# Value side first: reordering the work between the layers of a four-layer cross-attention kernel

## The reference, cut to what matters

```python
x = x + L0_xattn(layernorm(x), ctx, ...); x = x + L0_moe(layernorm(x), ...)    # top 2 of 8 experts
x = x + L1_xattn(layernorm(x), ctx, ...); x = x + L1_moe(layernorm(x), ...)    # top 1
x = x + L2_xattn(layernorm(x), ctx, ...); x = x + L2_ffn(layernorm(x), ...)    # gated, ternary weights
x = x + L3_xattn(layernorm(x), ctx, ...); x = x + L3_moe(layernorm(x), ...)    # top 1
# an attention: q = x @ Wq; k, v = ctx @ Wkv; softmax(q k^T * scale) v @ Wo + bo
```

## Time and profile before

| | us |
|---|---|
| median of 3 runs | 1031.07 (1029.62 to 1031.18) |
| profiled execution, whole | 1035.98 |
| its span, first to last instruction | 1033.6 |
| TensorE busy | 810.7 (78%) |
| VectorE busy | 600.9 (58%) |
| ScalarE busy | 485.4 (47%) |
| mean granted TensorE clock | 0.876 |

### The profile page before, as it was taken

The page is one execution under the profiler, slowest core; times in us unless marked ns, Lnnn a source line. Parts: engine busy times, 40 slices in busy tenths (PEclk is TensorE's granted clock), DMA queues, the critical chain, the costliest instruction groups (busy, mean ns, idle before and its releaser), DMA issues.

```text
span 1033.6 us, 15493 instructions
## 1 busy us (share of the span) xinstructions
PE 810.7 (78%) x4449; PEld 623.9 (60%) x4449; DVE 600.9 (58%) x2077; ACT 485.4 (47%) x1575; POOL 304.1 (29%) x396
## 2 busy tenths in 40 slices
PE   3887885599477888679956799889999777774794
PEld 1665675488345667557744577738668645563573
DVE  4756665487385788335436787452231258887574
ACT  2977752354175677124514445354443254441252
POOL 3100305367032355213401345300010113563142
PEclk9999987799797899669968899989999887885797
DMA  5032002333320000021110000000000300001213
GB/s 191 1 128 84 22 3 74 101 99 88 134 88 21 1 11 12 11 71 55 40 59 8 24 1 1 1 0 1 1 1 1 146 17 1 12 11 36 55 56 99
DMA packets 38642, 45.69 MB, mean 44 GB/s; under 512 B 7248, under 2 KB 31056, under 8 KB 37792
## 3 DMA queue, kind: packets, MB, share of 16 engines
q1 hardware_dynamic: 31344, 33.32, 10.0%
q0 software_dynamic: 4768, 9.91, 2.9%
q10 hardware_dynamic: 2448, 1.49, 0.5%
HBM read 31.92 MB, written 12.77 MB: 43 GB/s over the span
## 4 chain that ended last, share of the span: by engine, by line
PE 56%; DVE 24%; ACT 8%; issue 5%; DMA 4%; POOL 1%; SPq 1%; ACTq 0%; DVEq 0%; POOLq 0%
PE bank L940 8%; PE bank L834 7%; PE bank L897 6%; PE bank L915 5%; PE bank L807 5%; PE bank L832 4%; PE bank L767 4%; DVE s_xn L1082 3%; PE bank L818 3%; PE bank L906 3%; DVE s_peak L1105 2%; PE bank L756 2%; DVE s_total L1116 2%; PE bank L789 2%; ACT s_S L1572 1%
## 5 line engine op out<-in xcount | busy, mean ns | idle before, releaser
L807 PE MATMUL bank<-s_A,s_xTq 128*128 128x462 f32 (+1 forms) x352 | 157.6, 540 | 25.4 <-DVE s_S L1102 13.4
L1724 POOL TENSOR_TENSOR s_S<-s_S,s_inv 128x462 f32<-128x462 f32 (+1 forms) x128 | 105.1, 837 | 186.7 <-DVE s_inv L1119 185.4
L818 PE MATMUL bank<-s_ident,s_S 128*128 128x128 f32 (+2 forms) x560 | 97.4, 297 | 30.9 <-POOL s_S L1724 10.8
L818 PEld LDWEIGHTS bank<-s_ident,s_S 128*128 128x128 f32 (+2 forms) x560 | 71.6, 150 | 78.2 <-issue 37.2
L834 PEld LDWEIGHTS bank<-s_VW,s_PT 128*128 128x128 f32 (+2 forms) x800 | 111.7, 222 | 8.9 <-issue 7.7
L1757 POOL DMA_INDIRECT ys_L<-s_yo,s_yi x85 | 81.4, 957 | 121.3 <-DVE s_yo L1357 51.3
L834 PE MATMUL bank<-s_VW,s_PT 128*128 128x128 f32 (+2 forms) x800 | 114.4, 305 | 1.9 <-DVE s_x L1136 1.9
L1592 ACT ACTIVATE s_PT<-bank 128x384 f32<-128x384 f32 (+1 forms) x176 | 81.6, 470 | 64.6 <-PE bank L818 64.4
L789 PE MATMUL bank<-s_ident,s_xn 128*128 128x128 f32 x128 | 27.1, 353 | 84.3 <-DVE s_xn L1082 71.8
L1630 ACT ACTIVATE s_hT<-bank,s_b1T 128x128 f32<-128x128 f32 x184 | 52.7, 368 | 77.0 <-PE bank L906 76.9
L1750 POOL DMA_INDIRECT xs_L<-s_xn,s_sli x64 | 62.6, 977 | 88.8 <-DVE s_sli L1221 72.1
(11 more groups left out here) (214 smaller groups left out, 1733.0 us busy)
## 6 DMA issues: line engine op xcount, KB each, us to landing
s_xe<-xs_L SPq DMA_DIRECT2D x85, 66.0 KB
s_moe<-in_L_w SPq DMA_DIRECT2D x2, 2048.0 KB, 11.4
s_yb<-ys_L SPq DMA_DIRECT2D x16, 256.0 KB, 3.0
s_moe<-in_L_w SPq DMA_DIRECT2D x8, 512.0 KB, 7.0
s_arena<-in_L_w SPq DMA_DIRECT2D x2, 1024.0 KB, 5.9
s_arena<-in_L_h SPq DMA_DIRECT2D x2, 1024.0 KB, 9.1
ys_L<-s_yo,s_yi POOLq DMA_INDIRECT x85, 2.3
s_b2bc<-in_L_b SPq DMA_DIRECT2D x2, 512.0 KB, 5.8
```

What stands on the lines that cost most here:

```text
L807: mm(bank[b][:, 0:(h1 - h0) * KEYS], xTq_of(L, n)[:, i % 4, :], A[:, n, h0 * KEYS:h1 * KEYS], start=True, stop=True).then_inc(scores.up(L, ...
L818: w = turn(bank[b][0:m, P * (t - t0):P * (t - t0) + P], S[s][:, P * t:P * t + m], ident)
L1724: p.tensor_tensor(val, val, rep(inv[s][:, h0:h1], KEYS, 2), ALU.mult).then_inc(normed.up(L, i, k), 1)
```

## The change

For layers 2 and 3 (L = 1, 2) a new function `values_and_rows` writes the pieces in this order: the backs; products and folds of the value side; the combs; norm steps 0 and 1; three `vwt` pieces; norm steps 2 to 7; three `vwt` pieces; `xt`; the last six `vwt` pieces. The `vwt` pieces of these two layers are moved out by ScalarE for the first three batches and by VectorE for the last one; before, the two engines took them alternately. In the last layer this stays as it was. The attention's value matmuls wait for all pieces of their batch by name, where they waited for the last two.

For the last layer the key side is put alternately with norm and xt: product, norm step 0, fold 0, norm step 1, fold 1, norm step 2, and so on to fold 7, xt. The value side follows.

```diff
+    def values_and_rows(L):
+
+        side_work = keyside(L, 0)
+        vwt = [p for p in side_work if p[0] == "vwt"]
+        norm = [p for p in norm_rows("q", L, 0) if not isinstance(p, int)]
+        for piece in [*backs(L - 1, 0), *(p for p in side_work if p[0] != "vwt"), *combs(L - 1, 0), *norm[:2],
+                      *vwt[:3], *norm[2:], *vwt[3:6], ("xt", "q", L, 0), *vwt[6:]]:
+            put(*piece)
...
     experts(0)
-    woven(before(1, 0), [])
-    for piece in keyside(1, 0):
-        put(*piece)
+    values_and_rows(1)
     put("load", "L2v")
     put("load", "L2w")
...
     experts(1)
-    woven(before(2, 0), [])
-    for piece in keyside(2, 0):
-        put(*piece)
+    values_and_rows(2)
     put("load", "L3v")
...
     put("load", "L3w")
-    woven(before(3, 0), [])
-    for v in (1, 0):
-        for piece in keyside(3, v):
-            put(*piece)
+    woven(keyside(3, 1), before(3, 0))
+    for piece in keyside(3, 0):
+        put(*piece)
...
+    def on_dve_vwt(L, n, q):
+        return (n * len(spans(L)) + q) % 2 == 1 if L == 3 else n == NB - 1
...
-        mine = [(n, nq - 1), (n, nq - 2) if nq > 1 else (n - 1, 0)]
-        return [vwt_left(L, a, b) for a, b in mine if a >= 0]
+        return [vwt_left(L, n, q) for q in range(nq)]
```

More of the change, by code:

```diff
@@ L590, in body @@
     fold_dve = signal("fold_dve", (a for a in events("fold") if a[1] == 0 and a[2] % 2 == 0))
-    vwt_dve = signal("vwt_dve", (a for a in events("vwt") if (a[1] * len(spans(a[0])) + a[2]) % 2))
+    vwt_dve = signal("vwt_dve", (a for a in events("vwt") if on_dve_vwt(*a)))
     variance, scale_made, rows = signal("variance", "ln", 1), signal("ln_scale", "ln", 5), None
@@ L618, in body @@
     fold_act = signal("fold_act", (a for a in events("fold") if a[1] == 1 or a[2] % 2))
-    vwt_act = signal("vwt_act", (a for a in events("vwt") if not (a[1] * len(spans(a[0])) + a[2]) % 2))
+    vwt_act = signal("vwt_act", (a for a in events("vwt") if not on_dve_vwt(*a)))
     deviation = signal("deviation", "ln", 2)
@@ L688, in s_left @@
         return probs.at(L, i, k)
-    def on_dve_vwt(L, n, q):
-        return (n * len(spans(L)) + q) % 2 == 1
     def vwt_left(L, n, q):
```

## The result

The changed kernel took 998.42 us in the median (992.19 to 1000.27, 4 runs) against 1031.12 of the kernel before in the same comparison: a ratio of 0.9674, interval 0.9629 to 0.9719. The forecast was 1004.5: a gain of 26.6 us where 32.7 and then, by the second ratio, some 39 were measured. The time lies at the fast end of the range, that of the second ratio (0.9624 x 1031.12 = 992.4) beyond it.

A forecast was written before the change was run, and what follows sets the result against it. The prediction took TensorE's idle stretches in front of layers 2, 3 and 4 as the bound. Savings of 12.7 + 11.8 + 6.4, less 4.3 for the clock, gave 26.6 us: 1031.07 - 26.6 = 1004.5, range 998 to 1013.

The forecast's parts named there:

- What bounds the kernel: In front of layers 2, 3 and 4, TensorE stands idle (13.7 us at layer 2) before work that needs nothing of x.
- Products and folds straight behind the experts, at full clock: Layers 2 and 3: products follow the last expert matmul at once; first fold 3.11 us behind it.
- The transfer is hidden: Layers 2 and 3: fetched results land 2.7 and 5.4 us before VectorE asks for them, covered by the folds.
- Rows' transpose: Starts at 274.23 in layer 2; at 534.95 in layer 3, with 0.65 us lost to ScalarE's evictions.
- Scores in layers 2 and 3: First scores at 277.8 instead of 290.50 and 538.5 instead of 550.31, saving 12.7 and 11.8 us.
- the clock term: At the three starts, a lower granted clock costs between nothing and 12.8 us in all; a third, 4.3, was taken.
- Layer 4: Scores at 835.0 instead of 841.41, saving 6.4 us; table loads on the path, value product waits for fold evictions.
- that the attention would lose clock: Rival, slower: layer 2's attention at mean clock 0.65 takes 38 us more, time 1042; chance 0.04.
- the held clock: Rival: the clock holds throughout, all 30.9 us are kept, time 1000.2; chance 0.20.
- Late results: Rival: in layer 2 the fetch lands late, second addition 4.8 us later, time 1009.3; chance 0.07.
- a longer table load: Rival: in layer 4 ScalarE stands still as long again behind each load, 2.6 us, time 1007.1; chance 0.03.
- no gain: Rival: the attention does not follow its earlier start, something else setting its end, time 1031; chance 0.03.

The follow-up runs named there:

- the second ratio: The changed kernel run once more with no edit, against the kernel before: 995.54 us, ratio 0.9624.
- e8: The changed kernel, but SyncE issues the weight loads ahead of the fetches of the experts' results: 1004.77 us, ratio 0.9707.
- e1: The kernel before with the change made in front of layer 2 alone: 1021.22 us, ratio 0.9861.
- e7: The kernel before with three small unused VectorE additions behind the addition of fetched results in front of layer 3: 1029.54 us, ratio 0.9953.
- e9: The kernel before with six small unused VectorE additions behind the addition of fetched results in front of layer 3: 1030.2 us, ratio 0.9962.

## Why the prediction was right in its order and wrong in its size

- **What bounds the kernel:** right. The idle stretches, and most of the half clock behind them, are what the change removes: 30.1 us of gaps.
- **Products and folds straight behind the experts, at full clock:** right. The first fold came 261.77 - 258.99 = 2.78 us behind the last expert matmul, predicted 3.11; the two products overlap their copies, 2.06 us for both.
- **The transfer is hidden:** right; e8 shows what it costs when the cover is gone.
- **Rows' transpose:** 275.73 - 258.99 = 16.7 against 17.1 in layer 2. In layer 3 ScalarE delayed the logarithm by some 0.3 us where 0.65 was given.
- **Scores in layers 2 and 3:** predicted 20.6 us behind the last expert matmul in both, before the clock term. Measured 21.5 and 21.8 with the clock down in the value transposes, 20.0 to 20.2 with it up, and 19.5 in layer 3. The steps were some 0.5 us too dear in layer 2 with the clock up and 1.1 in layer 3: 0.3 of it in the products, 0.15 behind the rows' transpose (277.98 - 274.57 = 3.41 in e1 against 3.57), and in layer 3 another 0.35 in ScalarE's delay of the norm.
- **Layer 4:** predicted 19.3, measured 20.3 and, with the clock up, 18.9. The table loads were the bound, but by another way than predicted. The step said that the norm is done before the evictions and is not the bound. The evictions ended at 797.01 + 2.23 = 799.24, the rows' transpose behind the norm at 798.90 + 1.11 = 800.01, and the value product began at 799.95, behind it. That it came 9.6 us behind the gated network, where 825.2 - 815.72 = 9.5 was predicted, is in part luck. The exponential began at 796.90, at the end of its load (795.61 + 1.28), so no drain was paid here either; this agrees with the earlier trace rows and not with the Trainium skill (ScalarE: Activation LUTs, What ACT_TABLE_LOAD costs).
- **The clock term is the step that failed.** I took it as a cost only, between nothing and 12.8 us, put at 4.3, and looked for it at the three starts alone. There it cost 32.9 - 30.1 = 2.8 us in the first execution and 32.9 - 31.2 = 1.7 in the second (33.3 + 32.4 + 25.7 less 21.8 + 19.5 + 18.9 is 31.2). The sum took every stage behind the starts to keep its length, a term put at nothing without a reason: attentions 3 and 4 were 6.5 us shorter in the first execution and 8.8 in the second. Of the 32.7 - 26.6 = 6.1 us by which the first comparison exceeds the forecast, 2.0 lie in steps that came quicker (32.9 against 30.9), 4.3 - 2.8 = 1.5 in the clock at the starts, and 32.7 - 30.1 = 2.6 outside the gaps. Of the 39.0 - 26.6 = 12.4 of the second, the same terms hold 2.0, 2.6 and 7.8. The gaps are of one execution each and the times are medians, so these shares are rough; the largest is in both the one outside the gaps. The rows of before held a hint: a fall of the clock in an attention stood in the earlier trace rows, and I read it as something that stays where it is.
- **The rivals:** that the attention would lose clock had a later stage in view, as the runs do, but with the wrong sign. The time of the held clock, 1000.2, lies nearest to the measured 998.42; that is luck, since in the profiled execution the clock fell in front of layers 2 and 4. Late results, a longer table load, no gain and slower did not come about.

What stays open: how much of the gain in the attentions would remain under another shift. By e7 and e9 the kernel before runs 4 to 5 us faster with its order unchanged and a small delay, so a part of the measured ratio may not be owed to the new order. The part that is, counted in the gaps, is 30 to 33 us.

## What to carry to other kernels

Where two independent chains lie end to end behind an idle engine, put first the one that needs nothing new; price it from rows at full clock, and look for what then stands late in the queues (here a table load, which one moved line hid for another 2 to 3.5 us of the gap). A change that shifts all later work can also change which scant stretches, those with little work on TensorE, are followed by a fall of the granted clock, as e7 did: give the clock a term of both signs for every later stage with such stretches, not for the changed place alone. Before a gain of under 1% is credited to an edit, compare the lengths of the stages that it does not touch, and run the old kernel with a small delay.

## What the runs showed of the hardware that I had not expected

- With 0.94 us of added work in front of layer 3's norm the kernel was faster, ratio 0.9953 (0.9932 to 0.9975). Behind the same pieces and the same wait of 1.56 or 1.57 us the granted clock fell in three kernels and not in two others: 20 matmuls took 3.46, 3.48 and 3.83 us, or 2.40.
- Weights issued ahead of a scattered store lengthened that store's landing from 2.22 us (259.99 to 262.21 in the kernel before) to 5.58, and the fetch behind it from 3.41 to 7.84.
